# Node gathers and scatters on 127 partitions where the last has no node, in a graph network on one core

## The reference, cut to what matters

```python
def _gat(x, edge_index, W, att_s, att_d, bias, heads, ch, neg_slope):
    h = (x @ W.T).reshape(n, heads, ch)
    a_s = (h * att_s[None]).sum(-1)
    a_d = (h * att_d[None]).sum(-1)
    logits = jax.nn.leaky_relu(a_s[src] + a_d[dst], neg_slope)
    m = jax.ops.segment_max(logits, dst, num_segments=n)
    ex = jnp.exp(logits - m[dst])
    denom = jax.ops.segment_sum(ex, dst, num_segments=n)
    alpha = ex / (denom[dst] + 1e-16)
    out = jax.ops.segment_sum(alpha[:, :, None] * h[src], dst, num_segments=n)
    return out.reshape(n, heads * ch) + bias
...
x = _layernorm(x + L0(x))            # three _gat calls, elu and clip between them
e_feat = jnp.concatenate([x[rol], x[col], edge_attr], axis=-1)
v = jax.nn.relu(e_feat @ W1 + b1) @ W2 + b2
x_cand = jax.ops.segment_max(v, col, num_segments=num_nodes)
x = _layernorm(x + jnp.maximum(x_cand, x[:, -v.shape[-1]:]))
```

## Time and profile before

| | us |
|---|---|
| median of 3 runs | 16712.0 |
| lowest, highest | 16710.62, 16714.92 |
| span of the profiled execution | 16709.0 |
| POOL busy in it | 12580.8 |
| DVE busy in it | 9733.0 |
| PE busy in it | 5230.6 |

### The profile page before, as it was taken

The page is one execution under the profiler, slowest core; times in us unless marked ns, Lnnn a source line. Parts: engine busy times, 40 slices in busy tenths (PEclk is TensorE's granted clock), DMA queues, the critical chain, the costliest instruction groups (busy, mean ns, idle before and its releaser), DMA issues. The chain is left out here.

```text
span 16709.0 us, 72365 instructions
## 1 busy us (share of the span) xinstructions
PE 5230.6 (31%) x6238; PEld 1537.5 (9%) x6238; DVE 9733.0 (58%) x11755; ACT 2187.6 (13%) x4747; POOL 12580.8 (75%) x13328
## 2 busy tenths in 40 slices
PE   2333333332233333333223333333323333333332
PEld 1000000000000000000000000000000111111110
DVE  6666666666466666666546666666664444444445
ACT  2111111111011111111101111111111111111110
POOL 7777777777777777777777777777777777777777
PEclk9999999999999999999999999999995666666665
DMA  2111111111011111111101111111112222222222
GB/s 77 58 55 55 56 55 57 55 58 48 20 29 29 29 29 29 29 29 29 28 20 29 29 29 29 28 29 29 29 34 71 79 79 79 79 79 79 79 79 56
DMA packets 639804, 794.40 MB, mean 48 GB/s; under 512 B 252774, under 2 KB 418460, under 8 KB 627084
## 3 DMA queue, kind: packets, MB, share of 16 engines
q0 software_dynamic: 426768, 272.89, 8.8%
q1 hardware_dynamic: 99804, 295.38, 4.8%
q10 hardware_dynamic: 113184, 225.69, 3.7%
HBM read 442.63 MB, written 350.37 MB: 47 GB/s over the span
## 5 line engine op out<-in xcount | busy, mean ns | idle before, releaser
L589 POOL DMA_INDIRECT g<-table,idx x9375 | 8846.2, 944 | 2859.0 <-issue 2856.7
L692 PE MATMUL bank<-ad,ad_sel 4*128 4x512 f32 (+1 forms) x2352 | 2211.4, 1088 | 5306.7 <-DVE adf L1265 5306.7
L589 POOL DMA_INDIRECT g<-tablex,idx x3125 | 2948.4, 943 | 952.4 <-issue 952.4
L1255 DVE STREAM_TRANSPOSE h_sb<-g 128x512 f32<-128x512 f32 (+1 forms) x588 | 606.6, 1032 | 4002.1 <-DMA g<-table,idx 4002.1
L735 PE MATMUL bank<-d_b,w_out 128*128 128x512 f32 (+1 forms) x784 | 727.6, 1083 | 2462.0 <-ACT d_b L936 2462.0
L676 PE MATMUL bank<-r_in,qsel 4*128 4x512 bf16 (+2 forms) x784 | 444.0, 566 | 2875.9 <-issue 1841.0
L1352 DVE STREAM_TRANSPOSE bank<-g 128x512 f32<-128x512 f32 x196 | 142.1, 725 | 1940.8 <-DMA g<-tablex,idx 1940.8
L701 PE MATMUL bank<-h_sb,w_as 128*128 128x512 f32 x1176 | 1216.7, 1139 | 137.5 <-DVE h_sb L1255 137.5
L692 PEld LDWEIGHTS bank<-ad,ad_sel 4*128 4x128 f32 x2352 | 676.0, 316 | 6220.5 <-DVE adf L1265 5603.3
L754 ACT ACTIVATE idx<-idx_all 128x16 int32 (+1 forms) x784 | 168.7, 216 | 6149.2 <-DVE h_sb L1255 3873.2
L1265 DVE TENSOR_TENSOR_SCAN adf<-r_sb,adf,bank 128x512 f32<-128x512 f32 (+1 forms) x588 | 710.2, 1208 | 113.8 <-PE bank L692 113.8
(11 more groups left out here) (225 smaller groups left out, 7127.5 us busy)
## 6 DMA issues: line engine op xcount, KB each, us to landing
state<-o_sb ACTq DMA_DIRECT2D x582, 288.0 KB, 2.1
g<-table,idx POOLq DMA_INDIRECT x9375, 2.3
auxx<-wide SPq DMA_DIRECT2D x97, 1056.0 KB, 4.2
xd_in<-auxx SPq DMA_DIRECT2D x194, 512.0 KB
xe_t<-in_edge_attr SPq DMA_DIRECT2D x196, 256.0 KB
g<-tablex,idx POOLq DMA_INDIRECT x3125, 2.4
vmax<-o_sb ACTq DMA_DIRECT2D x194, 256.0 KB, 2.1
r_in<-rrow SPq DMA_DIRECT2D x776, 4.0 KB
```

The lines of the kernel that those rows point to most:

```text
L589: eng.indirect_dma_start(o, None, t[:, :], bass.IndirectOffsetOnAxis(ap=idx[k][:, j:j + 1], axis=0)).then_inc(e_g[k][j // (W // 2)], 16)
L692: last = eng.matmul(p_ad[:, 0:c], ad_sel[:, h, :], view(ad[b], h, [[2, c]], parts=NQ), start=(h == 0), stop=(h == 1))
L1255: v_.transpose(view(h_sb[b], 0, [[1, w], [w, SQ]]), view(g[k], 0, [[F, w], [1, F]])).then_inc(E["tin"], 1)
```

## The change

The gathers and scatters of columns 54 to 97 name partitions 0 to 126 only, in every node step. That is 44 of 98 gathers in each of steps 1 to 4, and 44 of 98 scatters in each of steps 0 to 3: 352 indirect transfers with 127 rows in place of 128. The 21st gather of `search`, and the counts, comparisons and the matmul that use it, take 16 partitions in place of 128. No instruction is added, removed or moved.

```diff
+KEND = P * NBLK + SAMPLES - (KT - 1) * P
...
+def node_parts(t):
+
+    return P if t < LAST_P else P - 1
+
+
+def pair_parts(t):
+
+    return P if t < KT - 1 else KEND
...
                 for t in range(KT):
                     eng.wait_ge(S["rowi"], t + 1)
-                    eng.indirect_dma_start(row_ids[t], None, dst_rows,
-                                           bass.IndirectOffsetOnAxis(ap=rowidx[:, t:t + 1], axis=0)).then_inc(q_row[t], 16)
+                    n = pair_parts(t)
+                    eng.indirect_dma_start(row_ids[t][0:n, :], None, dst_rows,
+                                           bass.IndirectOffsetOnAxis(ap=rowidx[0:n, t:t + 1], axis=0)).then_inc(q_row[t], 16)
...
                 for t in range(NT):
-                    eng.indirect_dma_start(ng[:, t, 0:w], None, src[:, :],
-                                           bass.IndirectOffsetOnAxis(ap=last_nm[:, t:t + 1], axis=0)).then_inc(n_g[t // TU], 16)
+                    n = node_parts(t)
+                    eng.indirect_dma_start(ng[0:n, t, 0:w], None, src[:, :],
+                                           bass.IndirectOffsetOnAxis(ap=last_nm[0:n, t:t + 1], axis=0)).then_inc(n_g[t // TU], 16)
...
                         at = u * TN + t
-                        o, i_ = (aux, td[:, at, :]) if step < 3 else (auxx, tdx[u][:, t, :])
-                        eng.indirect_dma_start(o[:, :], bass.IndirectOffsetOnAxis(ap=scat_nm[:, at:at + 1], axis=0),
+                        n = node_parts(at)
+                        o, i_ = (aux, td[0:n, at, :]) if step < 3 else (auxx, tdx[u][0:n, t, :])
+                        eng.indirect_dma_start(o[:, :], bass.IndirectOffsetOnAxis(ap=scat_nm[0:n, at:at + 1], axis=0),
                                                i_, None).then_inc(n_s[u], 16)
...
-                last = eng.matmul(p_start, sel_p[t], view(sel_v[t], t % 5 * NT, [[1, NT]]), start=(t == 0), stop=(t == KT - 1))
+                n = pair_parts(t)
+                last = eng.matmul(p_start, sel_p[t][0:n, :], view(sel_v[t], t % 5 * NT, [[1, NT]], parts=n), start=(t == 0), stop=(t == KT - 1))
...
+                n = pair_parts(t)
                 for j in range(BLK):
-                    count(row_ids[t], bound[:, t, j:j + 1], below[:, t, j:j + 1], L)
+                    count(row_ids[t][0:n, :], bound[0:n, t, j:j + 1], below[0:n, t, j:j + 1], L, parts=n)
```

More of the change, by code:

```diff
@@ L759, in _, with count @@
             n_sums = [0]
-            def count(x, bound_, o, width, scale=-1.0):
+            def count(x, bound_, o, width, scale=-1.0, parts=P):
                 n_sums[0] += 1
-                eng.activation(view(x1_nm, 2 * SAMPLES, [[1, width]]), x, ACT.Sign, scale=scale, bias=bound_, accum_out=o).then_inc(S["sums"], 1)
+                eng.activation(view(x1_nm, 2 * SAMPLES, [[1, width]], parts=parts), x, ACT.Sign, scale=scale, bias=bound_, accum_out=o).then_inc(S["sums"], 1)
                 eng.wait_ge(S["sums"], n_sums[0])
@@ L1031, in place @@
             def place(t):
-                v_.tensor_scalar(sel_p[t], miota[:, :], pair_p[:, t:t + 1], None, ALU.is_equal)
-                v_.tensor_tensor(view(sel_v[t], t % 5 * NT, [[BLK, NBLK], [1, BLK]]), view(is_i, t * NBLK, [[1, NBLK], [0, BLK]]),
-                                 view(below, t * BLK, [[0, NBLK], [1, BLK]]), ALU.mult).then_inc(S["sel"], 1)
+                n = pair_parts(t)
+                v_.tensor_scalar(sel_p[t][0:n, :], miota[0:n, :], pair_p[0:n, t:t + 1], None, ALU.is_equal)
+                v_.tensor_tensor(view(sel_v[t], t % 5 * NT, [[BLK, NBLK], [1, BLK]], parts=n), view(is_i, t * NBLK, [[1, NBLK], [0, BLK]], parts=n),
+                                 view(below, t * BLK, [[0, NBLK], [1, BLK]], parts=n), ALU.mult).then_inc(S["sel"], 1)
             def weights(l):
@@ L1061, in _ @@
                 tick(eng, "ticks2")
-                link(v_.tensor_scalar(below[:, t - 1, :], below[:, t - 1, :], 0.5, L / 2, ALU.mult, ALU.add))
+                n = pair_parts(t - 1)
+                link(v_.tensor_scalar(below[0:n, t - 1, :], below[0:n, t - 1, :], 0.5, L / 2, ALU.mult, ALU.add))
                 place(t - 1)
```

## The result

| | before | changed | difference |
|---|---|---|---|
| median of the runs, us | 16711.35 (4 runs) | 17407.65 (4 runs) | +696.3 |
| span of the profiled execution | 16709.0 | 17405.2 | +696.2 |
| POOL busy | 12580.8 | 13141.9 | +561.1 |
| DVE busy | 9733.0 | 9752.8 | +19.8 |

The ratio is 1.0416, with a 95% interval from 1.0401 to 1.0431. The change makes the kernel slower by 4.2%. The prediction was 16,708 us with a range from 16,690 to 17,150. The measured time lies outside it.

A forecast was written before the change was run, and what follows sets the result against it. POOL, issuing indirect transfers back to back, was taken to bound the kernel. Terms -2.6 + 0 - 1 = -3.6 us gave a 16,705.4 us span; with 3.0 us from span to median, 16,708.4 us, range 16,690 to 17,150.

The forecast's parts named there:

- What bounds the kernel: POOL's row, issuing indirect transfers back to back, is the time; each narrowed transfer's change moves the end 352 times.
- Issue of 352 transfers with 127 rows: POOL's issue of node gathers and scatters, columns 54 to 97: 7.4 ns less each, -2.6 us.
- Rival A: Issue of the 352 transfers on POOL gets longer, 127 addresses written for one engine; doubling, +332 us, 17,040; chance 0.31.
- Rival B: One fixed DMA engine takes all 127 rows, issue unchanged; step 4's last gather lands 53 us late, 16,761; chance 0.06.
- C: Issue of the 352 transfers on POOL gets shorter; at -0.15 us each -53 us, 16,656; chance 0.06.
- D: Issue works on all 128 partitions, leaving one out: 0 for the 352, 16,711 us; chance within the forecast's 0.57.
- The transfers themselves: Landing of narrowed gathers and scatters: slower landing costs once, in step 4; 0, or +2.3 us with one engine.
- the cover in steps 1 to 3: The last gathered tile has 84 scatters of earlier tiles ahead of its own, 106 us, hiding later landings.
- The 21st row gather: Prelude gather on 16 partitions: the table store may land sooner, shortening POOL's 2.28 us wait; -1 us.
- What would show it: Profile signs: issue medians of columns 54 to 97 (944 and 958 ns), packet counts, landings (2.4 and 2.1 us), prelude wait.

The follow-up runs named there:

- e1: Changed kernel with node scatters and the 21st row gather back at 128 partitions, so only node gathers take 127; 17,062.75 us, ratio 1.0209 to the kernel before.
- e2: Changed kernel with node gathers and the 21st row gather back at 128 partitions, so only node scatters take 127; 17,056.97 us, ratio 1.0206 to the kernel before.
- the ladder: Changed kernel with eleven widths from 126 to 16 rows, four columns each, in place of 127, and the 21st row gather at 128; 16,816.1 us (one run).
- e3: Changed kernel with all node gathers and scatters back at 128 partitions, only the prelude's 21st row gather narrowed to 16; 16,712.39 us against 16,712.38 before.

## Why the prediction was wrong

*What bounds the kernel* held. "What one of them gets longer or shorter by, the end moves by, 352 times" is what happened: 562 us more busy time and 132 us of stops on POOL's row are 694 of 696 us, and `e1` and `e2` each brought their half. That this is true of every node step held where the kernel before takes 16,712 us, and not in the sets where it takes 18,787.

*Issue of 352 transfers with 127 rows* is the step that failed. The term was put at -7.4 ns each, -2.6 us; it measured +1,600 ns each, +562 us, and stops on top. The value was taken "since 128 rows or 127, with no other difference, is what the nearest rows compare to". That is nearness in the number of rows. What counts is the number of rows on the fullest engine, and there 127 is the farthest from 128 that a count below it can be: 8 against 127. The prediction had worked out that case ("if the rows are shared out evenly over the 16 DMA engines only where that divides, all 127 go to one") and bounded it with +4,940 us, which took the whole 944 ns for proportional. By the ladder some 840 ns are fixed and 13.4 ns come with each row of the fullest share: (2,540 - 944) / 119. The rows used against it, POOL's `AFFINE_SELECT` on 4 and on 128 partitions, say something of arithmetic on POOL and nothing of the issue of a transfer.

*Rival A* was right in its direction, its place and its cause (127 rows for one engine where 8 each were shared by 16). Its size was not: a doubling, +332 us, was an estimate, and an issue 2.7 times as long, +562 us, with the stops made 696. It had no stops. The chance of 0.31 was low for a case that had a rule for it and no row against it. The range ended at an issue longer by 1.25 us, short of the 1.60 measured, so it would have been missed without the stops as well.

*Rival B*, one fixed engine that falls behind with the issue unchanged, did not occur: landings stay at 5.4 to 5.7 us over step 0's 44 scatters in a row. *C* (a shorter issue) and *D* (no effect) are out, by the 2.54 us.

*The transfers themselves*: put at 0, or +2.3 us with one engine. From the end of the last gather's issue to DVE's next instruction it is 3.0 us in place of 1.5, and at the end of the span 0.3 us are left of it. That step was right, and so was the cover in steps 1 to 3. Its picture of one busy engine and fifteen idle ones was not: the packets of a scatter take 20.8 us of engine time where 0.8 were reckoned, and by their sizes they are on all sixteen.

*The 21st row gather*: put at -1 us; 0.0 in `e3`. The wait it was to shorten varies between 2.3 and 4.7 us from profile to profile, whatever that gather's width.

*What would show it* named the right lines: the issue of the narrow transfers, the packets (48 for 32) and the landings (5.5 for 2.1 us) point to the cause.

## What to carry to other kernels

What an indirect transfer on GpSimd costs depends on the factors of its row count: choose a count that 16 divides, or one with a large divisor up to 16, and pad the last block with harmless rows. Here leaving out one padding row made each transfer 1.6 us dearer, and leaving out 16 brought 0.02 us. When a case that was worked out has a rule for it and no row against it, an instruction of that shape in a profile decides it, and until then its price belongs in the range. Whether a longer issue shows in the time depends on who else is waited for: the same 250 us on POOL were 248 where the kernel before took 16,712 us, and 73 to 92 where it took 18,787.

## What the runs showed of the hardware that was not expected

- The issue of an indirect transfer on POOL: 0.84 us for 1 row on the fullest engine, 0.94 to 0.98 for 7 to 9, 1.18 for 25, 1.31 for 31, 1.66 for 61, 2.36 for 113, 2.54 for 127.
- Read from packet sizes, for seven row counts: the queues of engines that get no data are filled with as many 4-byte entries as the fullest has rows. For 127 rows that is 508 bytes, 127 x 4, on each of fifteen engines.
- The landing goes with the same length: 2.1 us for 8 rows, 2.5 for 25, 3.5 to 3.8 for 61, 4.6 for 97, 5.5 for 127 (scatters of 8 bytes a row, and of 256).
- Stops of 2.2 to 3.9 us on POOL in long rows of transfers with 97 or more rows on one engine, mostly 7 or 14 transfers apart (once 12); cause open.
- Two levels of time for one kernel: the one before took 16,712 us in some sets of runs and 18,787 in others, 13 runs in each set, and chip number 7 stands beside both; cause open.
